# Sixteen query blocks built in token order on GpSimd, and one identity product fewer in each turn to the key layout

## The reference

```python
qkv = x @ w_qkv
q, k, v = to_heads(...)                 # 16 heads of 8 values
q = q * cos + _rotate_half(q) * sin     # and k likewise
att = jnp.einsum('bhtd,bhsd->bhts', q, k) * scale
att = jnp.where(causal, att, jnp.finfo(att.dtype).min)
att = jax.nn.softmax(att, axis=-1)
y = jnp.einsum('bhts,bhsd->bhtd', att, v)
return y.transpose(0, 2, 1, 3).reshape(B, T, C) @ w_proj
```

## Time and profile before

| | before |
|---|---|
| time, median of 3 (range) | 628.24 us (627.15 to 635.08) |
| the profiled execution, its span | 626.06 us, 624.3 us |
| PE, PEld | 565.9 us (91%), 401.8 us (64%) |
| DVE | 468.7 us (75%) |
| ACT | 337.6 us (54%) |
| POOL | 154.5 us (25%), 308 instructions |
| DVE's second product of the expert layers (L1166), 80 times | mean 704 ns |
| causal attention | from about 246 to 500 us of the span |

### The profile page before, as it was taken

The page is one execution under the profiler, slowest core; times in us unless marked ns, Lnnn a source line. Parts: engine busy times, 40 slices in busy tenths (PEclk is TensorE's granted clock), DMA queues, the critical chain, the costliest instruction groups (busy, mean ns, idle before and its releaser), DMA issues. The chain is left out here.

```text
span 624.3 us, 11755 instructions
## 1 busy us (share of the span) xinstructions
PE 565.9 (91%) x4072; PEld 401.8 (64%) x4072; DVE 468.7 (75%) x1493; ACT 337.6 (54%) x617; POOL 154.5 (25%) x308
## 2 busy tenths in 40 slices
PE   2996879989999987979999999988999998999997
PEld 1875768878877975655444454544454546888886
DVE  5577875597777775887888898889898334886764
ACT  4855447322223454466787777776777774223221
POOL 7810513120013453860504221213130000000000
PEclk9999979999999998568999999999999999999999
DMA  8000000033332210000000000000000003244342
GB/s 295 20 1 1 2 0 1 29 128 121 101 104 71 85 51 1 2 0 2 1 1 3 1 2 2 2 2 1 1 3 2 1 2 104 86 126 132 103 135 69
DMA packets 18666, 27.94 MB, mean 45 GB/s; under 512 B 2984, under 2 KB 7208, under 8 KB 18608
## 3 DMA queue, kind: packets, MB, share of 16 engines
q1 hardware_dynamic: 17888, 25.85, 13.0%
q10 hardware_dynamic: 720, 1.34, 0.7%
HBM read 25.85 MB, written 1.33 MB: 44 GB/s over the span
## 5 line engine op out<-in xcount | busy, mean ns | idle before, releaser
L870 ACT ACTIVATE arena<-bank 128x512 f32<-128x512 f32 x288 | 155.0, 602 | 53.8 <-PE bank L1713 32.4
L1235 DVE CUSTOM_DVE_ANT_0 bank<-bank,mask_qk 128x512 f32<-128x512 f32 (+3 forms) x256 | 116.9, 526 | 15.8 <-PE bank L1739 15.6
L1739 PE MATMUL bank<-kza,qta 64*128 64x512 f32 (+2 forms) x352 | 121.6, 445 | 6.9 <-DVE work L1238 3.5
L1695 PE MATMUL bank<-qtb,kza 64*128 64x512 f32 (+3 forms) x384 | 114.6, 397 | 3.1 <-DVE work L1235 2.5
L796 ACT ACTIVATE work<-bank 128x512 f32<-128x512 f32 x80 | 47.8, 598 | 110.5 <-PE bank L1359 110.3
L1739 PEld LDWEIGHTS bank<-kza,qta 64*128 64x128 f32 x352 | 58.9, 202 | 65.6 <-DVE work L1238 31.8
L1238 DVE TENSOR_REDUCE work<-bank 128x1 f32<-128x512 f32 x128 | 80.2, 683 | 14.4 <-PE bank L1739 14.4
L1162 DVE TENSOR_TENSOR work<-work,bank 128x512 f32<-128x512 f32 x80 | 54.7, 684 | 46.6 <-PE bank L1359 42.1
L1580 PE MATMUL bank<-dw,work 128*128 128x128 f32 x640 | 85.2, 277 | 0.9 <-DVE work L1166 0.9
L1580 PEld LDWEIGHTS bank<-dw,work 128*128 128x128 f32 x640 | 81.6, 192 | 5.1 <-issue 1.1
L1653 PE MATMUL bank<-arena 128*9 128x512 f32 (+3 forms) x768 | 77.8, 492 | 0.4 <-ACT arena L870 0.2
(11 more groups left out here) (190 smaller groups left out, 1029.4 us busy)
## 6 DMA issues: line engine op xcount, KB each, us to landing
kt<-cw_rows SPq DMA_DIRECT2D x160, 128.0 KB, 2.9
x<-x_in SPq DMA_DIRECT2D x4, 256.0 KB, 8.9
y_out<-x SPq DMA_DIRECT2D x4, 256.0 KB, 3.2
arena<-gw_in SPq DMA_DIRECT2D x1, 640.0 KB, 10.4
arena<-uw_in SPq DMA_DIRECT2D x1, 640.0 KB, 8.8
dw<-dw_in SPq DMA_DIRECT2D x1, 640.0 KB, 9.6
work<-q_in SPq DMA_DIRECT2D x2, 256.0 KB, 7.2
arena<-const_in ACTq DMA_DIRECT2D x1, 400.0 KB, 6.6
```

The source lines that it names most:

```text
L870: act.activation(dst, src, ACT.Exp, scale=SCALE).then_inc(p_ready, 1)
L1235: ins = dve.tensor_tensor_reduce(out=src, in0=src, in1=mask_qk[:, CW - w:], scale=1.0, scalar=-3e38, op0=ALU.add, op1=ALU.max, accum_out=dst)
L1695: ins = pe.matmul(s_bank(n)[:, at:at + w], kz(s, h, j // CT)[pair(h), j % CT * P:(j % CT + 1) * P], qtb[pair(h), s % 2, (c + 1) * CW - w:( ...
L1739: ins = pe.matmul(dst, qta[pair(h), slot(b, g), i * P:(i + 1) * P], keys, start=True, stop=True, skip_group_check=True)
```

## The change

The rotated queries are also kept in token order in plain float32 (`qtok`: the old `loc1` for sequence 0, a new tile `qtok1` for sequence 1), by one copy of 128x128 in each rotation: 12 on POOL, 4 on DVE. A new POOL task `fill`, 16 times, writes them into columns 0 to 23 of each head in `stm`: two rounding copies and a subtraction. PE's `maxima` waits for it (`stq_ready`), and its fifth product, L1632, is gone.

```diff
+    for half in range(2):
+        put("pool", -1, 0, "fill", 0, half)
     for t, k in enumerate(PREP):
         put("pool", -1, k, "rope", 1, t)
...
+    for s in range(1, STEPS):
+        for half, k in ((0, 0), (1, 2)):
+            put("pool", s - 1, k, "fill", s, half)
...
                 link(pool.tensor_tensor(a1[:, :, :], a1[:, :, :], a2[:, :, :], ALU.add))
+                pool.tensor_copy(qtok[b][:, i, :, :], a1[:, 0:H, :])
...
+            def fill(s, half):
+
+                n = 2 * s + half
+                b, g = divmod(s, G)
+                pool.wait_ge(*stg_done(TB * b + CT * half + CT - 1))
+                if n >= 2:
+                    pool.wait_ge(mx_full, n - 1)
+                q = qtok[b][:, half * CT:(half + 1) * CT, g * GH:(g + 1) * GH, :]
+                st = stm[:, half, :, :, :]
+                pool.tensor_copy(st[:, :, :, HD:2 * HD], q)
+                link(pool.tensor_copy(st[:, :, :, 0:HD], q))
+                pool.tensor_tensor(st[:, :, :, 2 * HD:3 * HD], q, st[:, :, :, 0:HD].bitcast(F32), ALU.subtract)\
+                    .then_inc(stq_ready, 1)
...
                 link(dve.tensor_tensor(a1[:, :, :], a1[:, :, :], a2[:, :, :], ALU.add))
+                dve.tensor_copy(qtok[0][:, i, :, :], a1[:, 0:H, :])
...
                 pe.wait_ge(stm_ready, n + 1)
+                pe.wait_ge(stq_ready, n + 1)
                 t_take(qtb_ready, n + 1)
 
-                b, g = divmod(s, G)
                 for t in range(CT):
-                    pe.matmul(T[:, t * P:(t + 1) * P], stm[:, half, t, :, :].rearrange("p h d -> p (h d)"),
-                              identr[:, :], start=(t == 0), stop=False, skip_group_check=True)
-                pe.matmul(T[:, :], identr[:, :], qta[:, slot(b, g), tok(half)], start=False, stop=True,
-                          skip_group_check=True).then_inc(mx_full, 1)
+                    ins = pe.matmul(T[:, t * P:(t + 1) * P], stm[:, half, t, :, :].rearrange("p h d -> p (h d)"),
+                                    identr[:, :], start=(t == 0), stop=(t == CT - 1), skip_group_check=True)
+                ins.then_inc(mx_full, 1)
```

More of the change, by code:

```diff
@@ L323, in macaron @@
         rden = work[:, o:o + 4 * H].rearrange("p (r e h) -> p r e h", r=2, e=2)
+        qtok1 = sb("qtok1", [P, S])
+        qtok = [q[:, :].rearrange("p (t h d) -> p t h d", t=TB, h=H) for q in (loc1, qtok1)]
         pb = arena[:, 0:2 * GH * CW].rearrange("p (r h n) -> p r h n", r=2, h=GH)
@@ L377, in macaron @@
         stm_ready, mx_full, qtb_ready = sem("stm_ready"), sem("mx_full"), sem("qtb_ready")
+        stq_ready = sem("stq_ready")
         b_full, p_ready, pv_done = sem("b_full"), sem("p_ready"), sem("pv_done")
@@ L644, in _ @@
                             alone(*todo[1:])
+                        if todo[0] == "fill":
+                            fill(*todo[1:])
                         if todo[0] == "norm":
```

## The result

| | before | after |
|---|---|---|
| time, median of 20 executions each | 629.08 us (625.86 to 635.08) | 623.61 us (621.58 to 628.09, and one of 707.79) |
| ratio, 95% interval | | 0.9914 (0.9888 to 0.9939) |
| the profiled execution, its span | 626.06, 624.3 us | 623.81, 622.0 us |
| POOL | 154.5 us, 308 instructions | 173.0 us, 368 instructions |
| PE matmuls | 4072 | 4056 |

The changed kernel is 5.5 us faster by the medians, 3.8 to 7.0 by the interval, and 2.3 us faster from profile to profile. The forecast was 625.0 us, with 0.92 on "within 2%".

A forecast was written before the change was run, and what follows sets the result against it. PE was taken to lead in the steady steps, DVE close behind. Terms -4.5 - 0.4 + 0.5 + 0.7 + 0.2 + 0.3 = -3.2 us took the median of 628.24 to 625.0 us, range 620.5 to 631.

The forecast's parts named there:

- The product: PE's fifth product behind the four turns of `stm`: removal gains 4.5 us for fifteen, 0.4 us for the first.
- The third wait: Added semaphore wait on PE at the turns of `stm`: 0.03 us each, +0.5 us, bound 0 to 1.6 us.
- The fills in steady steps: POOL's sixteen fills: 1.15 us each, `negate` of half 0 about 0.4 us later, nothing on the path.
- The longer rotations: Copy in each rotation on POOL or DVE: +0.7 us at tiles 14 and 15, +0.2 us at tile 7.
- Tile 7: Rotated on DVE; PE waits for it and starts step -1 behind it: +0.2 us, upper bound 0.29 us.
- The seven copies in the expert layer: Three on DVE, four on POOL, where PE never waited for POOL: nothing, at most 2.0 us.
- The rule of the two locked engines: DVE instructions on two SBUF operands and POOL's SBUF reads lock each other out: four copies, up to 1.2 us in all.
- Step -1: Two fills ahead of tile 8: PE waits 1.0 us at tile 9, slack uses it up; +0.3 us.
- (a): Rival, chance 0.20: DVE takes the lead, PE waits longer at its banks, gains are lost; about 628.5 us.
- (b): Rival, chance 0.16: fills ahead of tile 8 delay PE and prolong half clock in step -1; 629.3 to 631.6 us.
- (c): Rival, chance 0.12: the turn ends earlier, `T` and `qtb` come free earlier, clock returns one stretch earlier; 621 us.

The follow-up runs named there:

- product_out: Kernel before with the identity product gone and nothing in its place, query rows left out of the scores; ratio 0.9971, attention -4.51 us.
- product_x3: Kernel before with the identity product done three times in a row; ratio 1.0101, attention +6.56 us.
- fills_beside: Changed kernel with the identity product put back, third wait, fills and copies kept; 628.78 us, ratio 1.0005, attention +0.89 us against the kernel before.
- copy_last: Changed kernel with each copy to `qtok` moved behind the four writes of the staging tile; 633.08 us, ratio 0.9994.
- fills_later: Changed kernel with the two fills of step 0 moved behind the rotations of tiles 9 and 11; 624.25 us, ratio 0.9917.
- same_before: Kernel before, run again unchanged against itself; 628.74 us, ratio 0.9998.
- same_after: Changed kernel, run again unchanged, against the kernel before; 624.18 us, ratio 0.9919.
- both_later: Changed kernel with the fills of step 0 behind tiles 9 and 11 and each copy behind the staging writes; 634.99 us, ratio 1.0041.

## Why the prediction was right, step by step

- **The product.** Forecast 4.5 + 0.4 = 4.9 us; measured 4.51 (`product_out`), 0.28 for each of the fifteen at full clock and 0.3 for the first, in step -1. The distance between starts fell by 0.30 per turn in the trace of after (0.89 to 0.59). The two sums by the figures of the Trainium skill (TensorE: Matmul & The Clock Gate, Back-to-back issue gap), 2.1 and 3.5 us for sixteen, were too low. Even in a run of three, a product of 512 columns cost 0.23 us here (`product_x3`), near its isolated figure and not its sustained one.
- **The third wait.** Forecast 0.5, bound 1.6 us; measured nothing: 0.59 us against 0.58 in L1663, and `fills_beside` stands still over 150 us with eleven such waits. This is the term that was mis-sized most: it was 0.5 too high, the product 0.4 too high the other way, and the rotations of tiles 14 and 15 0.2 too high, and together that makes -3.6 of -3.2.
- **The fills in steady steps.** Forecast 1.15 us each and hidden; measured 1.01 and hidden. `negate` of half 0 stood 0.4 us later by forecast; it began at 349.74 where it was 349.24. Behind `fill` it has no idle time ahead of it (POOL of after; the turn that needs it starts at 354.75, 4.2 us behind its end):

```profile
348.71 0.29 POOL L584 CAST stm<-loc 128x128 fp32r<-128x128 f32 x1
349.74 0.26 POOL L604 TENSOR_SCALAR work<-work 128x16 f32<-128x16 f32 x1
350.36 0.23 POOL L608 TENSOR_TENSOR stm<-work,stm 128x16 fp32r<-128x16 f32 x1
```

- **The longer rotations.** Forecast 0.35 at each of tiles 14 and 15; measured 0.23 and 0.25 (the distance from L584 to L585, 0.23 us, is what a copy of that size adds in POOL's queue; its own 0.29 us overlap with the next). Tile 7: forecast 0.2; PE's wait grew by 0.13 us, from 1.46 to 1.59, and hardly any of it lasted (0.04 us in `copy_last`). The seven copies in the expert layer cost nothing: `fills_beside` lost 0.06 us from 190 to 241 us. But their own price was wrong. POOL's four took 0.64 to 0.68 us there and not 0.29, each beside DVE's product of two operands in SBUF and each ending 0.15 us behind it, and the product of the earlier trace rows took 1.22 us instead of 1.12 (trace of after):

```profile
207.65 1.22 DVE L1192 TENSOR_TENSOR work<-work,kt 128x512 f32<-128x512 f32 x1
208.39 0.64 POOL L539 COPY loc<-arena 128x128 f32<-128x128 f32 x1
```

The rule of the two locked engines, which the prediction has from the Trainium skill (SBUF — State Buffer, SBUF: two separate sides), agrees with this trace. But it cost the stage nothing, so the 1.2 us that the prediction put at its upper end did not come.
- **Step -1.** Forecast 0.3 us, and 0.2 for tile 7, with the delay used up by slack; measured 0.48 for the two together (`fills_beside`), and 0.40 came back when the fills were moved (`fills_later`). The way there was partly another: the wait at tile 9 was 0.41 us and not 1.0, because PE was itself 0.4 us late, and the delay then went through ACT, which copies tile 9, makes four key copies and only then frees `T` for PE: the wait of 1.09 us at 263.95. I had looked only at PE and DVE there.
- **The rivals.** (a), DVE taking the lead, is refuted: 61.2 against 61.6 us of waits. (b)'s mechanism at tile 9 is there at its small price; half clock ended at about 287 us as before. (c), an earlier free `T`, is not to be seen: the gain is the product's alone. Two prices were off by their own terms: all of the 4.5 us lost gives 629.5 in (a), not 629.7, and (c)'s 621 has a source for 1.7 of its 4 us.
- **The median.** It lay 5.5 us below that of before, the attention 3.6 to 3.8. The forecast change of -3.2 us was right for the attention, and lies outside the measured interval of 3.8 to 7.0; that 625.0 us was met within 1.4 us is in part luck, as the median of before rose from 628.24 to 629.08 with more executions. The rest, 1.9 us with an interval of 0.2 to 3.4, isn't explained by the change. The traces show where such amounts come from: the two of the changed kernel differ by 3.0 us ahead of 210 us, the two of before by 1.6 us at 520. The granted clock of the executions points there too: its mean is 0.9601 in the changed kernel and 0.9577 in the kernel before (as run beside `same_before`), which over 624 us is 1.5 us at most, by my estimate. But with `same_after` the two are 0.9589 and 0.9580, so this stays open.

## What to carry to other kernels

A product of 512 columns that stands between two others was worth its distance between starts here, 0.28 to 0.30 us, and not its busy time of 0.45; look for the same sequence without it elsewhere in the trace. Work moved to an engine with three quarters of its time free cost something here only where that engine was waited for in order, so put it behind the write that others wait for, and follow the delay through every engine that shares the bank. Before crediting or blaming a change of half a per cent, compare one stage between two fixed instructions: executions of one kernel differ by more than that where the clock falls at a seam. And make sure that the granted clock is alike within the stage.

## What the runs showed of the hardware that I had not expected

A kernel can lose 9 to 13 us (1.5 to 2%) to one fall of TensorE's granted clock at a seam where PE issues tiny products and waits, with PE marked 9.5 us busy of 10: in `both_later` 24 us and in `copy_last` 34 us at 0.50, though each has a shorter attention than the changed kernel. Some 8 us of useless products did not make `both_later` slower: over all executions its median went from 634.99 to 631.18 us, by the ratios it stayed where it was.

An extra semaphore wait on a matmul, for something long done, cost under 0.02 us (eleven of them in `fills_beside`). On POOL a cast of 128x128 to rounded float32 took 0.29 us, with 0.23 between starts, and a subtraction of that size 0.46. A copy of that size took 0.29 us on POOL in the attention and 0.64 to 0.68 in the expert layer, beside DVE.
